# Attention scores and weighted sums in half rows of the array, the keys of a sum taken in two turns

## The reference, cut to what matters

```python
# x: (4, 2048, 256), 8 heads of 64, one k and one v for all heads
xn = layernorm(x)
q = l2norm((layer_norm(xn, norm_g) @ Wq) heads) * 4
k = l2norm(layer_norm(xn, norm_g) @ Wkv[:, :64]) * 4
v = layer_norm(xn, norm_g) @ Wkv[:, 64:]
sim = einsum('bhid,bjd->bhij', q, k)
out = softmax(sim) @ v                 # per head
s = layer_norm(out @ Wout, out_norm_g)
...
# top 2 of 8 experts with a capacity: gather rows, gelu(x @ w1 + b1) @ w2 + b2,
# times the gate, summed back into the rows
g = silu(moe(xn))
return x + s * g
```

## Time and profile before

| | us |
|---|---|
| runs of the kernel | 2847.08, 2844.91, 2851.07 (median 2847.08) |
| profiled execution, its own time | 2851.47 |
| its span, first to last instruction | 2849.7 |
| PE busy in the span | 2706.8 (95%) |
| DVE busy | 2045.8 (72%) |
| ACT busy | 1827.0 (64%) |

### The profile page before, as it was taken

One profiled execution on the slowest core, in us unless ns is written; L12 is line 12 of the kernel. 1 busy time (PEld: TensorE's weight loads), 2 busy tenths in 40 slices (PEclk: granted clock), 3 DMA queues, 4 the chain that ended last, 5 costly groups with the idle time before them and its releaser, 6 DMA issues.

```text
span 2849.7 us, 84972 instructions
## 1 busy us (share of the span) xinstructions
PE 2706.8 (95%) x37573; PEld 1792.3 (63%) x37637; DVE 2045.8 (72%) x3077; ACT 1827.0 (64%) x2355; POOL 642.8 (23%) x428
## 2 busy tenths in 40 slices
PE   4999999998989999999999999999999999999996
PEld 3666666665655665666666666676666666666664
DVE  5888888989867783334334334338999999999986
ACT  6877777766655665545545455447777777777763
POOL 3111111113767310000000000002344343433312
PEclk8999999999999999999999999999999999999997
DMA  3223222102423102223222313111112121111101
GB/s 104 87 80 119 76 87 95 44 28 65 143 96 107 54 10 61 63 67 84 74 62 78 82 53 84 53 40 32 34 52 60 49 61 45 53 45 52 43 21 44
DMA packets 207649, 184.07 MB, mean 65 GB/s; under 512 B 99048, under 2 KB 185008, under 8 KB 207280
## 3 DMA queue, kind: packets, MB, share of 16 engines
q1 hardware_dynamic: 194992, 145.06, 17.1%
q0 software_dynamic: 12288, 33.57, 3.7%
HBM read 71.61 MB, written 85.98 MB: 55 GB/s over the span
## 4 chain that ended last, share of the span: by engine, by line
PE 82%; ACT 7%; DVE 5%; issue 5%; DMA 1%; POOL 0%; SPq 0%; POOLq 0%; ACTq 0%; DVEq 0%
PE pair L598 24%; PE bank L655 14%; PE pair L641 13%; PE bank L618 8%; PE bank L626 7%; PE bank L616 7%; PE bank L579 3%; PE bank L537 2%; ACT arena L807 2%; DVE arena L1151 2%; PE bank L549 1%; ACT h_f L814 1%; PE bank L567 1%; PE bank L506 1%; ACT oT L689 0%
## 5 line engine op out<-in xcount | busy, mean ns | idle before, releaser
L1151 DVE TENSOR_TENSOR arena<-arena 128x1024 bf16<-128x1024 f32 (+1 forms) x1032 | 1221.6, 1212 | 198.4 <-ACT arena L807 182.1
L807 ACT ACTIVATE arena<-pair 128x1024 f32<-128x1024 f32 (+1 forms) x1032 | 1017.5, 1017 | 364.6 <-PE pair L598 341.8
L598 PE MATMUL pair<-qT,kT 128*128 128x512 f16 (+1 forms) x4096 | 885.4, 384 | 39.6 <-ACT arena L807 34.1
L616 PE MATMUL bank<-vhl,arena 128*128 128x65 bf16 x8192 | 649.7, 193 | 7.0 <-DVE att L1144 3.8
L618 PE MATMUL bank<-vhl,arena 128*128 128x64 bf16 x8192 | 650.9, 195 | 4.4 <-issue 4.4
L616 PEld LDWEIGHTS bank<-vhl,arena 128*128 128x128 bf16 x8192 | 567.9, 99 | 58.9 <-issue 4.5
L618 PEld LDWEIGHTS bank<-vhl,arena 128*128 128x128 bf16 x8192 | 549.7, 97 | 57.8 <-issue 7.0
L598 PEld LDWEIGHTS pair<-qT,kT 128*128 128x128 f16 (+1 forms) x4096 | 201.4, 96 | 491.3 <-issue 418.9
L814 ACT ACTIVATE h_f<-pair,b1T 128x512 f32<-128x512 f32 x320 | 218.9, 684 | 382.8 <-PE pair L641 382.2
L1200 POOL TENSOR_TENSOR q_small<-q_small,minus_half 128x8 f32<-128x8 f32 x64 | 150.8, 2356 | 1341.6 <-DVE q_small L1064 1341.6
L626 PE MATMUL bank<-vhl,arena 128*128 128x65 bf16 x8192 | 422.5, 194 | 9.6 <-issue 7.6
(11 more groups left out here) (188 smaller groups left out, 1913.9 us busy)
## 6 DMA issues: line engine op xcount, KB each, us to landing
routed_rows<-h_f SPq DMA_DIRECT2D x80, 256.0 KB, 4.5
expert_rows<-att SPq DMA_DIRECT2D x40, 512.0 KB, 2.8
raw<-in_L_ffn_w SPq DMA_DIRECT2D x32, 512.0 KB
xn_rows<-s_hl SPq DMA_DIRECT2D x16, 512.0 KB, 2.9
xT_out<-xn_rows SPq DMA_DIRECT2D x64, 128.0 KB
w_lo<-in_L_attn_x SPq DMA_DIRECT2D x64, 128.0 KB
out<-w_lo SPq DMA_DIRECT2D x64, 128.0 KB
s_xin<-in_L_attn_x SPq DMA_DIRECT2D x12, 512.0 KB, 5.2
```

The lines of the kernel that those rows point to most:

```text
L598: t = nc.tensor.matmul(into, kT[g // BG % 2][rows, part, keys], qT[g % 2][rows, h, :], start=(turn == 0), stop=(turn == 1))
L616: nc.tensor.matmul(bank[:, at:at + DH + 1], p_top[:, s, cols, 1], V[:, kb, 0:DH + 1], start=(kb == 0 and qb == 0), stop=False, skip_group_ ...
L807: nc.scalar.activation(p_f32[:, n % NP, columns(n)], pairs[n % 2][:, columns(n)], ACT.Exp).then_inc(exped, 1)
L1151: nc.vector.tensor_tensor(p_lo[:, n % NP, c], p_f32[:, n % NP, c], p_top[:, n % NP, c, 1], ALU.subtract).then_inc(lowed, 1)
```

## The change

**Queries.** `qhl` is laid out so that after the transposes one slice of `qT` holds the high parts of an even and an odd head above each other, and the next slice their low parts. **Scores.** All three products are 64 rows long: the even head in the upper 64 rows of the array, the odd head in the lower 64. A step has six matmuls of 64 rows and 512 columns instead of two of 128 and two of 64 rows.

**Weighted sums.** `weigh(n, turn)` takes the 128 keys in two halves of 64. In turn 0 the even head uses the upper 64 rows and the odd head the lower 64; in turn 1 they change over. A turn has 24 matmuls of 64 or 65 columns, so a step has 48 instead of 24; the two heads alternate from matmul to matmul. The sums go to the same banks. A new semaphore `half_weighed` counts the turns 0; turn 1 of two steps waits until their turn 0 is over, and turn 0 of two steps until turn 1 of the two before is over, both on PE's own matmuls.

**Order.** In every slot PE now has the scores of one step and then one turn of two steps. `LAG` is 5 instead of 3, and the ring has 6 slots instead of 5.

```diff
-NP = 5
-LAG = 3
+NP = 6
+LAG = 5
...
             if b is not None:
-                place["weigh", b] = at + b % 2
-                weighed_in[at + b % 2].append(b)
+                place["weigh", b] = at - b % 2
+                weighed_in[at - b % 2].append(b)
...
-        qhl = sb("qhl", [P, H // 2, 4, DH], F16)
-        q_his, q_los = qhl[:, :, 0:4:3, :], qhl[:, :, 1:3, :]
+        qhl = sb("qhl", [P, H // 2, 2, 2, DH], F16)
+        q_his, q_los = qhl[:, :, 0, :, :], qhl[:, :, 1, :, :]
...
                 pe.wait_ge(exped, n - 1)
-                for turn in range(2):
+                for k_part, q_part in ((0, 0), (0, 1), (1, 0)):
                     for i, g, h, kb in halves(n):
                         into, keys = pairs[n % 2][:, i * BANK:(i + 1) * BANK], slice(kb * P, (kb + 1) * P)
-
-                        part = (turn + n) % 2
-                        rows = slice(i * DH, (i + 1) * DH) if part else slice(0, P)
-                        t = nc.tensor.matmul(into, kT[g // BG % 2][rows, part, keys], qT[g % 2][rows, h, :],
-                                             start=(turn == 0), stop=(turn == 1))
+                        rows = slice(i * DH, (i + 1) * DH)
+                        t = nc.tensor.matmul(into, kT[g // BG % 2][rows, k_part, keys],
+                                             qT[g % 2][rows, h // 2 * 2 + q_part, :],
+                                             start=(k_part + q_part == 0), stop=(k_part == 1))
...
-            def weigh(n):
+            def weigh(n, turn):
+
                 s = n % NP
+                if turn:
+                    pe.wait_ge(half_weighed, n - n % 2 + 2)
+                else:
+                    pe.wait_ge(weighed, n - n % 2)
                 pe.wait_ge(exped, n + 1)
...
+                for qb in range(GT):
+                    at = qb * (DH + 1)
+                    for width, of in ((DH + 1, 0), (DH, DH + 1)):
+                        for i, g, h, kb in halves(n):
+                            V, bank = vhl[g // BG % 2], acc_banks[(g * H + h) % 3]
+                            rows = slice((i + turn) % 2 * DH, ((i + turn) % 2 + 1) * DH)
+                            cols = slice(i * BANK + qb * P, i * BANK + (qb + 1) * P)
+                            nc.tensor.matmul(bank[:, at:at + width], p_top[rows, s, cols, 1],
+                                             V[rows, kb, of:of + width],
...
-                    if a is not None and a % 2 == 0:
+                    if a is not None:
                         scores(a)
-                        scores(a + 1)
+                    for n in weighed_in[clock.now + 1]:
+                        weigh(n, 0)
                     for n in weighed_in[clock.now]:
-                        weigh(n)
+                        weigh(n, 1)
```

More of the change, by code:

```diff
@@ L285, in build_program @@
         PAIR = 2 * BANK
-        arena = sb("arena", [P, 32 * 1024], mybir.dt.uint8)
+        arena = sb("arena", [P, NP * PAIR * 6], mybir.dt.uint8)
         p_f32 = arena[:, 0:NP * PAIR * 4].bitcast(F32).rearrange("p (n c) -> p n c", n=NP)
@@ L354, in build_program @@
                              "q_hi", "q_lo", "q_turned", "qT_copied")]
-        scored, exped, lowed, weighed = [sem(n) for n in ("scored", "exped", "lowed", "weighed")]
+        scored, exped, lowed, half_weighed, weighed = [sem(n) for n in (
+            "scored", "exped", "lowed", "half_weighed", "weighed")]
         head_inv, divided = sem("head_inv"), sem("divided")
@@ L620, in weigh @@
-                pe.wait_ge(lowed, n + 1)
-                for i, g, h, kb in halves(n):
-                    V, bank = vhl[g // BG % 2], acc_banks[(g * H + h) % 3]
-                    for qb in range(GT):
-                        at = qb * (DH + 1)
-                        cols = slice(i * BANK + qb * P, i * BANK + (qb + 1) * P)
-                        t = nc.tensor.matmul(bank[:, at:at + DH + 1], p_lo[:, s, cols], V[:, kb, 0:DH + 1],
-                                             start=False, stop=(kb == KB - 1), skip_group_check=True)
@@ L628, in weigh @@
-                t.then_inc(weighed, 1)
+                for qb in range(GT):
[7 more added lines that the diff above has]
+                                             V[rows, kb, of:of + width],
+                                             start=(kb == 0 and qb == 0 and turn == 0 and of == 0), stop=False,
+                                             skip_group_check=True)
@@ new lines, in weigh @@
+                pe.wait_ge(lowed, n + 1)
+                for qb in range(GT):
+                    at = qb * (DH + 1)
+                    for i, g, h, kb in halves(n):
+                        V, bank = vhl[g // BG % 2], acc_banks[(g * H + h) % 3]
+                        rows = slice((i + turn) % 2 * DH, ((i + turn) % 2 + 1) * DH)
+                        cols = slice(i * BANK + qb * P, i * BANK + (qb + 1) * P)
+                        t = nc.tensor.matmul(bank[:, at:at + DH + 1], p_lo[rows, s, cols], V[rows, kb, 0:DH + 1],
+                                             start=False, stop=(kb == KB - 1 and turn == 1), skip_group_check=True)
@@ L630, in first_layer @@
+                t.then_inc(weighed if turn else half_weighed, 1)
             def first_layer(fg, f):
```

10 lines of the change are left out of this document (2 added, 8 removed).

## The result

| | before, us | after, us |
|---|---|---|
| median of the runs | 2845.99 (4 runs, 2841.47 to 2851.07) | 2920.52 (4 runs, 2915.73 to 2921.14) |
| ratio | | 1.0258, 95% interval 1.0237 to 1.0279 |
| span of the profiled execution | 2849.7 | 2919.4 |

What follows compares the result with a forecast made beforehand. PE, busy 95% of the span, was taken as the bound. Scores, switches and weighing net -47, waits -22, supply +15 and DVE +2 made -52 us from 2851.5, adjusted to a median of 2797 us; range 2755 to 2960 us.

Steps and rivals of the forecast that it cites:

- The scores' term: Scores on PE: three pairs of half-row matmuls without change of shape, 0.107 us less per step, -111 us over 1032 steps.
- The switches: Transposes and projections, full-row work now alone among half rows at 295 places: 0.215 us each, +63 us.
- 24 matmuls become 48: Weighing on PE: a pair of half-row matmuls fits into one full-row matmul's 30.8 ns, no change.
- (b): Rival, weighing: the 25.6 ns pace of small matmuls holds for the whole engine, +506 us, 3290 us; chance 0.14.
- (c): Rival, weighing: no overlap of the halves with few columns, +764 us, 3545 us; chance 0.05.
- (a): Rival, weighing: each pair a few nanoseconds longer; at 5 ns +124 us, 2920 us; chance 0.22.
- Instruction supply, +15 us: PE's "issue" gaps in the weighing between 598 and 946 us double with the number of instructions: +15 us.
- I cost them at nothing: PE's new waits for `weighed` and `half_weighed`: what they wait for ended at least 0.65 us earlier, so no cost.
- A lower granted clock in the attention: Sign in the attention that would show the forecast wrong; no size was given.
- Waits for exp: PE's waits at the scores, 34.1 us in all: two thirds given back by the new order, -22 us.
- DVE's floor: From 2070 to 2692 us DVE's 594.2 us of work and half its idle time leave 602 us: +2 us.
- 'issue' gaps throughout the weighing: Sign in PE's weighing that would show the forecast wrong; no size was given.

Runs made afterwards that it cites:

- ref_after_c: The changed kernel, unaltered, in a group where semaphore updates were on time: 2839.27 us, 1.0078 times the kernel before (2814.79 us).
- a_merged_alt: Changed kernel with exp's two high-part products in one 128-column matmul and the row halves' order turned round every second pair of steps: 2777.20 us, 0.9864 times the kernel before.
- b_merged: Kernel before with the two products of exp's high part made by one 128-column matmul, 16 instead of 24 weighing matmuls per step: 2805.19 us, ratio 0.9850.
- e_quiet: Changed kernel with 24 of 80 blocks of zeros written and the last stage's gathers as plain DMAs from fixed rows: 2897.00 us, 1.0152 times the kernel before.
- ref_after_b: The changed kernel, unaltered, in a group where semaphore updates were late: 2940.83 us, 1.0320 times the kernel before (2852.38 us).
- b_pad52: Kernel before with 55,466 more instructions, long-fulfilled waits ahead of the matmuls of scores and weighing: 7712.05 us, 2.7081 times the kernel before.
- b_ownwait: Kernel before with a wait for PE's own `weighed` count ahead of `weigh`, in the midst of a slot: 2899.32 us, 1.0299 times the kernel before.

## Why the prediction was wrong

The three sums by start to start that follow, scores -117, full-row work +48 and weighing +135 us, make +66 of the +70 us by which the span grew. The first two came near the forecast. The third was put at nothing, with 15 us for supply.

**The scores' term held.** From start to start, all scores of the attention took 850.3 us before and 733.2 after, 117.1 less; the forecast had 111, and some of its 22 us of waits falls in here too.

**The switches held.** A full-row matmul behind half rows starts 0.12 us after the last of them and not 0.03, a half-row one behind full rows 0.15 and not 0.06: 0.19 us per place against the 0.215 forecast, at 292 places. Full-row work took 280.0 us instead of 231.7; the way from half to full rows, 0.09 of the 0.19 us, lies in the weighing's sum.

**24 matmuls become 48: the pace held, the term did not.** A pair takes 30.8 ns wherever the row runs through. Of the rivals, (b) and (c) are refuted by this, and so is (a), though its 2920 us is the time that was measured: it puts a few nanoseconds on every pair, and the trace has none on the pairs and whole microseconds between some of them. That the measured time fell on (a)'s number, and inside the range of 2755 to 2960 us only by (a)'s share of it, is luck. The weighing took 798.2 us before and 933.4 after; intervals of over 60 ns hold 40.6 and 169.7 us of that, the rest differs by 6 us in 50,000 matmuls.

**The step that failed first: "Instruction supply, +15 us".** The prediction saw "issue" gaps between 598 and 946 us and doubled those. It took the wrong rows for the cause. The gaps of the kernel before are hardly at fetches (1.5 of the 28.8 us between 600 and 950 us end 1.1 to 1.7 us after a packet), and the page's q8 row, 295 packets for 2850 us, was read over. The shortage appears in a stretch that had next to no pauses before: in the weighing from 57 to 600 us 2.0 before and 26.0 after, of which 24.3 end 1.1 to 1.7 us behind a packet. Over the whole trace of the result the pauses between matmuls of the weighing grew from 31.5 to 101.2 us, those behind a packet from 1.8 to 43.4. Where updates are on time, supply stands by itself. 2797 of 2847 is 0.982; ref_after_c is 1.0078; the difference is 2.5% of 2815, 72 us, and the trace has 82.4 us of pauses in the weighing, 70.2 behind a packet. So supply was worth three to five times the 15 us put down for it (43.4 and 70.2 us).

**The second: "I cost them at nothing", of the waits for `weighed` and `half_weighed`.** What they wait for was indeed issued 0.65 us earlier. The prediction took issue for arrival. Where updates are late the waits show 29.5 us, and the loss grows from 0.8 to between 2.6 and 3.2%, another 50 to 70 us. With one of the two waits taken away it is 2.0% in one such group. How the rest divides between these waits, the later `scored` for ACT, the pauses in a row and the clock stays open.

**A term that the forecast's sum does not have: the clock.** Beside long pauses the trace shows the granted clock at its lower level: the pause shown above ran to 240.2 us, and the clock was at 1.2 GHz from 239.8 to 243.2 us, and the weighing's matmuls started some 27 ns apart there instead of 15. Over the trace of the result it was at that level for 143.5 us, before for 108.6. After the change 1122 matmuls of the weighing stand in such time, each some 15 ns dearer, and 160 of the scores, each 0.11 us dearer, 34 us together; before it is 240 at 24 ns and 43 at up to 0.2 us, some 14. The difference, some 20 us, is an estimate of what the clock cost, in part as a consequence of the pauses, in part because the full clock begins at 82.7 instead of 71.9 us. "A lower granted clock in the attention" stood among the prediction's signs and came, weakly.

**Waits for exp** fell by 20.5 us, 22 were forecast. But where before 46 intervals between scores were over 0.6 us (51.1 us) and 7 are now (5.1), 38 such intervals (47.3 us) now stand between a step's scores and its weighing. The wait went and another came to the next border.

**DVE's floor** did not matter, because PE never came down to it. It comes nearer in a_merged_alt, where PE waits for L1161 for 23.1 us.

**The forecast's own signs** were right and misread in weight: "'issue' gaps throughout the weighing" stood there as what would show it wrong, and that is what came; but no rival had them as its mechanism, and none had a chance.

**A better kernel?** b_merged, 0.9850, is faster than both, but leaves out what it says: the low sums aren't added, and the last column of v's low part is not formed. Adding them would cost DVE work in the stretch where it is at its floor. It was not run, so no faster kernel of equal precision is shown here.

**Two small slips in its sums** change nothing above. 24 columns at 0.216 us for 512 are 10.1 ns, two fifths of the 25.6 ns and not a third. And the chances of (a), (b) and (c) add up to 0.41, against 0.38 for "slower".

## What to carry to other kernels

Count instructions as a resource: when an edit doubles the number of small matmuls at equal array time, compare the packets of the instruction queue over the span, and find the stretch where they are wanted fastest beside the heaviest traffic. Cost a wait by when the update arrives and not by when the work was issued, also on an engine that waits for itself. And run the unaltered changed kernel beside every group of experiments: three edits here seemed to win two points that belonged to the conditions of the group.

## What the runs showed of the hardware

- Matmuls of 64 rows and 64 or 65 columns that alternate between the two halves of the rows start every 15.4 ns for 48 in a row, in pairs 3 to 5 ns apart. Full-row matmuls in a row came no closer than 25.6 ns in the kernel before, with 24 and 16 columns.
- A packet of q8 holds 16 KB and comes for every 255 of TensorE's instructions. With one every 4.0 us, PE pauses for 82 us of 2842 within its rows of small matmuls, 70 of them until 1.1 to 1.7 us after a packet has landed (ref_after_c); with one every 7.8 us it pauses so for 1.8 us (the kernel before).
- TensorE's semaphore updates can arrive some 5 us after the matmul that raises them, beside GpSimd's indirect DMAs and in four of six groups of runs only. Those of ScalarE's exp and VectorE's `low` were never late in any trace, as far as it has them. With plain DMAs of the same size in the place of the gathers, one update is late where some 180 were (e_quiet, ref_after_b).
- A wait instruction that is long fulfilled costs TensorE's queue 88 ns on average (b_pad52); a wait for the matmul just issued 0.16 us (b_ownwait).
- A change between full and half rows costs about 0.09 us each way where small matmuls stand on both sides (0.12 instead of 0.03 us and 0.15 instead of 0.06).
- Near the end of a pause of 3 us TensorE's granted clock went from 2.4 to 1.2 GHz for 3.4 us, and the same half-row matmuls started some 27 instead of 15 ns apart (after, from 239.8 us on).
